# Two attention loops: projections two batches ahead, router logits kept in SBUF, and another split of the copies of turned probabilities

## The reference, cut to what matters

```python
x = x + tanh(g_xattn[0]) * attention0(layernorm(x), ctx, ctx, mask)      # mask: one for all batches
x = x + tanh(g_ffn[0])   * experts0(layernorm(x))                        # 64 experts, 6 of them for a token
x = x + tanh(g_xattn[1]) * attention1(layernorm(x), ctx, ctx, bias)      # bias: 128 x 120 for each batch
x = x + tanh(g_ffn[1])   * experts1(layernorm(x))                        # 8 experts, each picks 1024 tokens
# attention: q = n @ wq, k = ctx @ wk, v = ctx @ wv; softmax(q k' / sqrt(8) + mask or bias) v; @ wo
# router of either mixture: softmax(layernorm(x) @ gate)
```

## Time and profile before

| what | value |
|---|---|
| median of three runs | 928.5 us |
| profiled execution: its span | 930.0 us |
| busy: TensorE, VectorE, ScalarE, GpSimd | 716.6, 691.5, 473.2, 615.0 us |
| loop of layer 0, 142.75 us from 96.39: TensorE, VectorE, ScalarE, GpSimd busy | 131.86, 131.65, 118.68, 98.04 us |
| loop of layer 1, 163.11 us from 479.26: the same | 153.29, 151.98, 120.35, 136.07 us |
| first scores and last transpose of an output in layer 0's loop | 18.68 and 265.65 us |
| first scores and last transpose of an output in layer 1's loop | 405.20 and 669.72 us |
| granted TensorE clock in both loops | 1.00 of full speed |

### The profile page before, as it was taken

How to read it: one execution, slowest core, us unless ns; L and a number is a source line. 1 busy time by engine, 2 the same in 40 slices (tenths; PEclk the granted TensorE clock), 3 DMA queues, 4 the chain that set the end, 5 groups by cost and what they waited for, 6 DMA issues and landing times. The chain is left out here.

```text
span 930.0 us, 23773 instructions
## 1 busy us (share of the span) xinstructions
PE 716.6 (77%) x6259; PEld 491.8 (53%) x6259; DVE 691.5 (74%) x2257; ACT 473.2 (51%) x1687; POOL 615.0 (66%) x1109
## 2 busy tenths in 40 slices
PE   3888999999947998258999999999711379879770
PEld 1555566556623666236666666666501256567550
DVE  3787999999966664148999999999878756765334
ACT  2886888888831222037777777777500033423220
POOL 4888666666643676467888888887300466777772
PEclk9999999999977999679999999999955599999895
DMA  5211222222113333134344434443100216655568
GB/s 164 77 50 69 78 76 78 79 79 92 71 59 102 105 105 104 47 103 136 126 145 134 132 124 139 143 143 106 59 9 1 81 48 173 179 163 166 163 180 240
DMA packets 98731, 100.61 MB, mean 108 GB/s; under 512 B 24511, under 2 KB 76077, under 8 KB 98659
## 3 DMA queue, kind: packets, MB, share of 16 engines
q1 hardware_dynamic: 88306, 88.25, 30.5%
q0 software_dynamic: 6656, 9.66, 3.7%
q10 hardware_dynamic: 3696, 1.84, 0.7%
HBM read 60.84 MB, written 44.17 MB: 113 GB/s over the span
## 5 line engine op out<-in xcount | busy, mean ns | idle before, releaser
L574 ACT ACTIVATE P<-bank,mx 128x120 f32<-128x120 f32 x1024 | 277.5, 430 | 70.3 <-DVE mx L876 70.3
L473 PE MATMUL bank<-ident,P 128*120 128x128 f32 x1024 | 167.2, 286 | 28.7 <-ACT P L574 24.0
L473 PEld LDWEIGHTS bank<-ident,P 128*120 128x120 f32 x1024 | 106.1, 138 | 116.7 <-issue 70.7
L876 DVE TENSOR_REDUCE mx<-bank 128x4 f32<-128x480 f32 x256 | 150.3, 649 | 21.2 <-PE bank L455 18.1
L1761 POOL DMA_INDIRECT xg<-token_rows,tokens x64 | 66.8, 1044 | 70.8 <-DVE tokens L1815 51.9
L446 PE MATMUL bank<-bp,identr 128*128 128x480 f32 x256 | 87.5, 428 | 0.0
L1771 POOL DMA_INDIRECT expert_sums<-y,sum_rows x64 | 72.8, 1137 | 22.2 <-issue 19.2
L491 PE MATMUL bank<-PT,Vb 120*32 120x128 f32 x2048 | 82.9, 280 | 5.1 <-DVE PT L884 4.5
L676 POOL TENSOR_TENSOR Km<-Kf,kmask 128x480 f32<-128x480 f32 x64 | 63.2, 987 | 28.2 <-ACT Kf L558 27.4
L641 POOL TENSOR_TENSOR rstd<-rs,minus_half 128x1 f32<-128x1 f32 x128 | 73.1, 571 | 10.7
L455 PE MATMUL bank<-Km,qf 32*128 32x480 f32 x512 | 70.9, 623 | 3.0 <-POOL Km L676 2.9
(11 more groups left out here) (244 smaller groups left out, 1678.7 us busy)
## 6 DMA issues: line engine op xcount, KB each, us to landing
expert_sums<-zeros SPq DMA_DIRECT2D x32, 512.0 KB, 3.4
choice_rows<-zeros SPq DMA_DIRECT2D x32, 384.0 KB, 2.4
yrows<-choice_rows SPq DMA_DIRECT2D x32, 384.0 KB, 3.1
XT<-expert_sums SPq DMA_DIRECT2D x16, 512.0 KB, 6.3
XS<-expert_sums SPq DMA_DIRECT2D x16, 512.0 KB, 6.1
w<-in_w13T SPq DMA_DIRECT2D x8, 704.0 KB, 4.2
token_rows<-payload SPq DMA_DIRECT2D x32, 128.0 KB, 1.7
ctx<-in_ctxT SPq DMA_DIRECT2D x64, 60.0 KB, 2.0
```

Source lines behind the costliest of these rows:

```text
L473: mm = nc.tensor.transpose(TB[r % 2][0:KV, S * j:S * j + S], t.P[:, r, j, :], t.ident[:])
L574: e = nc.scalar.activation(t.P[:, r, j, :], heads(SC[r])[:, j, :], ACT.Exp, bias=t.mx[:, G * r + j:G * r + j + 1], scale=-1.0)
L876: ve.tensor_reduce(t.mx[:, G * r:G * r + G], heads(SC[r]), AX.X, ALU.min).then_inc(ev.mins, 1)
```

## The change

In `step` of TensorE the transposes of batch b+2 and of the router's b-3 go right behind `turn(before, 3)` (`small_transposes`). The projection, now of batch b+2 instead of b+1, and the logits, now of b-3 instead of b-4, go behind the second bias (`small_products`), where the transposes were. In the first two steps of layer 1 (`starting`) the transposes go behind the fourth product with the values instead.

ScalarE copies the transposes between the exponentials of groups 2 and 3, and after the exponentials of group 4 come the router's exponential, the copy of turned group 2, a copy of the logits to SBUF (`keep_logits`, a new operation), the copies of q, k and v, and the copy of turned group 3. VectorE copies turned groups 1 and 4 in both layers, group 4 right behind the router's maximum. The router's maximum and exponential read the logits in SBUF; their tiles have four buffers instead of two. VectorE no longer copies turned group 2 and goes from `turn_back` (layer 0: and `number0`) to `residual`; `router_invert` moves in between the two instructions of the second statistics. In the set-up two semaphores go away.

The core of the diff (the `used` waits, buffer indices and tile sizes that only follow from this are cut):

```diff
@@ TensorE
             def turn(b, r):
                 pe.wait_ge(ev.exped, G * b + r + 1)
-                if L == 1:
...
+                if r == 0:
+                    used(pe, ev.pt_act, 2 * b)
+                elif r == 1:
+                    used(pe, ev.pt_dve, 2 * b)
+                elif r == 2:
+                    pe.wait_ge(ev.pt_dve, 2 * b + 1)
                 else:
-                    pe.wait_ge(ev.pt_dve, 2 * b + r - 1)
+                    pe.wait_ge(ev.pt_act, 2 * b + 1)
@@
+                if r in (0, 3):
+                    pe.wait_ge(ev.pt_dve, 2 * b + 1 + r // 3)
                 else:
-                    pe.wait_ge(ev.pt_act, 2 * b + r - 1)
+                    pe.wait_ge(ev.pt_act, 2 * b + r)
@@
+            def small_transposes(i, k):
+                u, w = k % 2, (k + 1) % 2
+                if on(i, 1) is not None:
+                    pe.wait_ge(ev.v_kept, on(i, 1) + 1)
+                if on(i, -4) is not None:
+                    pe.wait_ge(ev.logits_kept, on(i, -4) + 1)
+                if on(i, 2) is not None:
+                    transpose_x(on(i, 2), u)
+                if on(i, -3) is not None:
+                    transpose_x2(on(i, -3), (k + 1) % 4)
+
+            def small_products(i, k):
+                u, w = k % 2, (k + 1) % 2
+                if on(i, -3) is not None:
+                    pe.wait_ge(ev.xT2c, on(i, -3) + 1)
+                if on(i, 2) is not None:
+                    project(on(i, 2), u)
+                if on(i, -3) is not None:
+                    logits(on(i, -3), w)
+
             def step(i, k):
+                starting = L == 1 and isinstance(i, int) and i <= 1
                 if before is not None:
                     turn(before, 3)
-                if on(i, -4) is not None:
-                    pe.wait_ge(ev.xT2c, on(i, -4) + 1)
-                if after is not None:
-                    project(after, w)
-                if on(i, -4) is not None:
-                    logits(on(i, -4), u)
+                if not starting:
+                    small_transposes(i, k)
@@
                     values(before, (k + 3) % 4, 3)
+                if starting:
+                    small_transposes(i, k)
                 if here is not None:
                     turn(here, 1)
                 if after is not None:
                     biases(after, w, 1)
-                    used(pe, ev.v_kept, after + 1)
-                if on(i, -4) is not None:
-                    pe.wait_ge(ev.rexp, on(i, -4) + 1)
-                if on(i, 2) is not None:
-                    transpose_x(on(i, 2), u)
-                if on(i, -3) is not None:
-                    transpose_x2(on(i, -3), (k + 1) % 4)
+                small_products(i, k)
                 if here is not None:
                     turn(here, 2)
@@ ScalarE
+            def keep_logits(b, v):
+                act.wait_ge(ev.logits, b + 1)
+                used(act, ev.rexp, b - 3)
+                used(act, ev.negmax, b - 3)
+                nc.scalar.activation(t.lg[:, v, 0:sc_w], lg_ps, ACT.Copy).then_inc(ev.logits_kept, 1)
@@
             def step(i, k):
-                if L == 0 and on(i, -1) is not None:
-                    keep_turned(on(i, -1), 3)
                 if here is not None:
                     exponentials(here, 0)
                     exponentials(here, 1)
-                if on(i, 1) is not None:
-                    keep_projections(on(i, 1), w, (k + 1) % 4)
-                if on(i, -4) is not None:
-                    router_exp(on(i, -4), u)
-                if here is not None:
-                    exponentials(here, 2)
-                    exponentials(here, 3)
-                    keep_turned(here, 2)
                 if on(i, -3) is not None:
                     act.wait_ge(ev.xT2, on(i, -3) + 1)
                 if on(i, 2) is not None:
                     copy_x(on(i, 2), u)
                 if on(i, -3) is not None:
                     copy_x2(on(i, -3), w)
+                if here is not None:
+                    exponentials(here, 2)
+                    exponentials(here, 3)
+                if on(i, -4) is not None:
+                    router_exp(on(i, -4), k)
+                if here is not None:
+                    keep_turned(here, 1)
+                if on(i, -3) is not None:
+                    keep_logits(on(i, -3), (k + 1) % 4)
+                if on(i, 2) is not None:
+                    keep_projections(on(i, 2), u, (k + 2) % 4)
+                if here is not None:
+                    keep_turned(here, 2)
@@ VectorE, layer 0 (layer 1 has keep_turned(before, 3) here already)
                 if s4 is not None:
-                    router_max(routed, u)
+                    router_max(routed, k)
+                if before is not None:
+                    keep_turned(before, 3)
@@ VectorE, both layers
                 if s1 is not None:
                     turn_back(before, w, s1)
-                if here is not None:
-                    keep_turned(here, 1)
...
                 if s1 is not None:
                     residual(before, w)
+                    first_stats2(before, s1)
+                if s4 is not None:
+                    router_invert(routed, k, s4)
+                if s1 is not None:
+                    last_stats(w, 1, ev.stats2, s1)
```

More of the change, by code:

```diff
@@ L184, in setup_block @@
     t.tokens_loaded, t.rest_loaded = sem("tokens_loaded"), sem("rest_loaded")
-    numbered, slots_made = sem("slots_numbered"), sem("slot_numbers_made")
-    consts_made, perm_made, permuted = (sem(x) for x in ("key_masks_made", "order_made", "biases_ordered"))
+    numbered = sem("slots_numbered")
+    perm_made, permuted = (sem(x) for x in ("order_made", "biases_ordered"))
     first = [
@@ L552, in keep_projections @@
                 act.wait_ge(ev.qkv, b + 1)
-                if on_logits(b) is not None:
-                    act.wait_ge(ev.negmax, on_logits(b) + 1)
                 used(act, ev.k_heads, b - 1)
@@ L564, in keep_projections @@
                     v_ps.rearrange("p (g r d) -> p g r d", g=2 * G, r=2), ACT.Copy).then_inc(ev.v_kept, 1)
-            def on_logits(b):
-                return b - 5 if not isinstance(b, int) or b >= 5 else None
             def exponentials(b, r):
@@ L598, in copy_x2, with router_exp @@
                 nc.scalar.activation(t.xT2[:, u, :], xT2_ps, ACT.Copy).then_inc(ev.xT2c, 1)
-            def router_exp(b, u):
+            def keep_logits(b, v):
[3 more added lines that the diff above has]
+                nc.scalar.activation(t.lg[:, v, 0:sc_w], lg_ps, ACT.Copy).then_inc(ev.logits_kept, 1)
+            def router_exp(b, v):
                 act.wait_ge(ev.negmax, b + 1)
-                used(act, ev.payload, b - 1)
+                used(act, ev.payload, b - 3)
                 if L == 0:
-                    used(act, ev.shares, b - 1)
-                nc.scalar.activation(t.ex[:, u, 0:sc_w], lg_ps, ACT.Exp, bias=t.negmax[:, u, :],
-                                     accum_out=t.exsum[:, u, :]).then_inc(ev.rexp, 1)
+                    used(act, ev.shares, b - 3)
+                nc.scalar.activation(t.ex[:, v, 0:sc_w], t.lg[:, v, 0:sc_w], ACT.Exp, bias=t.negmax[:, v, :],
+                                     accum_out=t.exsum[:, v, :]).then_inc(ev.rexp, 1)
             def step(i, k):
@@ L918, in residual, with first_stats2, router_max, router_invert @@
                                         ALU.add).then_inc(ev.resid, 1)
-            def stats2(p, u, c):
+            def first_stats2(p, c):
                 Apart.wait(dve, ev.resid, p + 1)
-                stats(p, u, 1, ev.stats2, c)
-            def router_max(p, u):
-                dve.wait_ge(ev.logits, p + 1)
-                ve.tensor_reduce(t.negmax[:, u, :], lg_ps, AX.X, ALU.max, negate=True).then_inc(ev.negmax, 1)
-            def router_invert(p, u, c):
+                first_stats(p, 1, ev.stats2, c)
+            def router_max(p, v):
+                dve.wait_ge(ev.logits_kept, p + 1)
+                used(dve, ev.rexp, p - 3)
+                ve.tensor_reduce(t.negmax[:, v, :], t.lg[:, v, 0:sc_w], AX.X, ALU.max, negate=True).then_inc(ev.negmax, 1)
+            def router_invert(p, v, c):
                 dve.wait_ge(ev.rexp, p + 1)
                 if L == 0:
-                    used(dve, ev.shares, p - 1)
-                c.note(ve.reciprocal(t.exrec[:, u, :], t.exsum[:, u, :]))
-            def biased0(p, u, v, c):
+                    used(dve, ev.shares, p - 3)
+                c.note(ve.reciprocal(t.exrec[:, v, :], t.exsum[:, v, :]))
+            def biased0(p, v, c):
                 c.settle()
-                c.note(ve.scalar_tensor_tensor(t.biased[:], t.ex[:, u, :], t.exrec[:, u, :], t.gb[:], ALU.mult, ALU.add))
+                c.note(ve.scalar_tensor_tensor(t.biased[:], t.ex[:, v, :], t.exrec[:, v, :], t.gb[:], ALU.mult, ALU.add))
             def top0(p, c):
@@ L960, in number0, with router1 @@
```

(15 more changed lines are left out.)

44 lines of the change are left out of this document (14 added, 30 removed).

## The result

The changed kernel took 975.16 us (median of five runs, 970.41 to 976.67) against 929.42 us for the kernel before (five runs beside it, 928.15 to 934.57). The ratio is 1.043, with an interval of 1.039 to 1.047. I had forecast 944 us and a range up to 956. The sign was right; the size was three times mine. The profiled execution took 970.41 us with a span of 968.7, against 930.0 before: +38.7 us to place. It is the fastest of the five and has the highest mean granted clock (0.899, the others 0.891 to 0.894); the medians are 45.7 apart, so about 7 us of a typical execution are not placed here.

A forecast was written before the change was run, and what follows sets the result against it. Layer 0 bound by ScalarE's chain, layer 1 by the ring over VectorE and TensorE. Layer 0 4.8, jumps 1.0, start 1.3, layer 1 6.2 and 1.7, drains 0.5: +15.5 on the 928.5 median gives 944 us, range 931 to 956.

The forecast's parts named there:

- the place of the products: Layer 1, TensorE: products behind the wait for group 4 lengthen the step to 8.37 against 8.06, 0.31 more.
- their price: Products on TensorE: 0.88 us for eight float32 passes, 0.11 us each, kept over 0.65 from the skill's 81 ns.
- VectorE's relief: Layer 1: VectorE sheds about 0.65 with the copy of turned group 2; nothing helps, as it then waits for the projection.
- the bracket of 0.8: Sign in layer 1: a wait of about 0.8 instead of 0.18 shown on TensorE's product of group 4.
- The products move behind the second bias: Deciding step, TensorE: second bias to turn of group 3 goes from 0.98 to 1.40 in layer 1; layer 0 grows 0.20.
- a wait at the small transposes for v: Sign that the forecast is wrong: TensorE waiting at the small transposes for v; no size given.
- (a): Rival, faster: ScalarE's exponentials' ring was what counted; layer 0 about 6.9, layer 1 7.75, kernel 905 us; chance 0.11.
- (b): Rival, no measurable change: products cost 0.6 as weights load while TensorE waits for group 4; kernel 931 us; chance 0.14.
- (c): Rival, slower still: ScalarE's last copies, of v and group 3, become the ring; 0.3 more a step, 960 us; chance 0.07.
- Ends: Starts and ends of both attention loops: layer 0's start 1.3 later, layer 1's start 0; bounds 0 to +4.
- GpSimd's 2.2 us of relief in layer 1: Layer 1's start: GpSimd no longer idles 3.88 for the keys of batch 2, of which 2.2 counted as saved.
- the drains: Loop ends: two steps with projections longer, the last without shorter, +0.5 in sum for both layers.

The follow-up runs named there:

- q three times: Changed kernel with layer 1's projection of q made three times in place instead of once: ratio 1.056 to the kernel before, layer 1's inner step 8.81.
- products early: Changed kernel with GpSimd's router normalisation first and, in layer 1, products ahead of group 1's turn and ScalarE's transpose copies ahead of the exponentials: ratio 1.007.
- router's root first: Changed kernel with GpSimd in layer 0 making the router's normalisation ahead of the one for the queries: ratio 1.020 to the kernel before.
- wait filled: Changed kernel with six useless matmuls on TensorE ahead of the router's transpose in layer 0: 975.84 us, ratio 1.044 to the kernel before.
- split only: Kernel before with only the new copy split, ScalarE copying turned groups 2 and 3, VectorE 1 and 4: ratio 0.997, layer 0 7.29 a step.

## Why the prediction was wrong

Right, and shown: the place of the products sets layer 1 (q three times, products early), their price is 0.11 a pass, VectorE's relief bought nothing, and the step grew by 0.31. Measured there: group 4's product, biases and projections within 0.1 of every forecast time. That the step came out at 8.37 exactly was luck: the output projection came 0.1 earlier (the products take 0.80, not 0.88), the residual 0.1 later behind it than the 0.42 from the earlier trace rows. And the bracket of 0.8 that I had named as a sign stood at the turn of group 1.

Right in layer 0, once the wait is gone: 7.58 and 7.59 where I had 7.69, so the change without the wait costs 0.14 a step in the mean (7.51 to 7.65), where I had 0.20. The split alone gives 0.22 back, so the move by itself costs 0.36 there.

**The failed step** is "The products move behind the second bias", where it says "What leaves this stretch is the pair of small transposes". I counted what they free and never asked what they wait for where they go. I took the router's tokens of b-3 as long ready, as they were at M+4.2, and among the signs I named a wait at the small transposes for v, which would have come from ScalarE, but not one for GpSimd. I followed v and the logits to their writers, and not the tokens. What it cost in layer 0, first to last transpose:

| term | from | us |
|---|---|---|
| products and split, no wait | router's root first less before, 237.1 - 232.9 | 4.2 |
| the wait itself, at full clock | wait filled less router's root first, 254.1 - 237.1 | 17.0 |
| low clock behind it | after less wait filled, 260.4 - 254.1 | 6.3 |
| sum (rounded) | | 27.4 |

The first row was forecast with 5.8, the other two with nothing. The middle row takes the filling as free, which the unchanged 8.31 supports, and the rows compare profiles from different chips, where equal loops of layer 0 agreed within 1 us.

Rivals: (a), faster by ScalarE's ring, did not come, since TensorE stayed behind the copy of group 4; but its premise was real, -0.22 in "split only". (b), cheap products, is refuted by 0.44 for four passes. (c), ScalarE's tail, did not bind (in the step of layer 0 shown above ScalarE stands idle for 1.58 us ahead of its exponentials); its price gave no more than 960 either. None had a wait for GpSimd. Ends: the first outputs came 2.0 later, not 1.3, and layer 1's start and end gave 9.3 - 20 x 0.31 = 3.1 for all steps outside the hardware loop, against 2.2 with its share of the drains. GpSimd's 2.2 us of relief in layer 1 can't be seen apart.

## What to carry to other kernels

Where a change moves an instruction earlier, look up in the trace of before when each of its operands was finished, by the writer's row, and compare it with the new place: slack of 2 us in the old place says nothing about the new. In an engine that works in order, the wait is paid by all that stands behind it, so put work that waits for nobody ahead of it, or change the order on the engine that is late; either took away 23 to 24 us here. Work made for a later batch belongs where the engine would wait anyway, ahead of the wait and not behind it.

## What the runs showed of the hardware

A gap of 1.66 us in a step of 8.3, with TensorE busy for the rest, was enough for the granted clock to fall to 0.50 in some steps and not in others, 27.2 us in all in layer 0 in either profile. Of the steps where it fell, most were 1.2 to 1.5 us longer from M to M than the same step with the wait filled, and the next one 0.4 to 0.8 shorter. With gaps of 0.56 and 0.47 in a step of 7.6 (router's root first) the clock was 1.00 over 160 us of the loop. So the low clock adds about a third to what the wait itself costs here (6.3 on 17.0 us), and which steps pay differs from one execution to the next.
